# A graph attention and message kernel: VectorE adds a step's sums to its block one step later in its program

## The reference

```python
h = jnp.maximum(_layernorm(x), 0.0)
Q, K, V = (h @ Wq), (h @ Wk), (h @ Wv)            # each (6250, 8 heads, 32)
score = einsum('ehd,ehd->eh', Q[dst], K[src]) / sqrt(32) + relu(efeat @ W1 + b1) @ W2 + b2
m = segment_max(score, dst)
ex = exp(score - m[dst])
denom = segment_sum(ex, dst)
out = segment_sum((ex / denom[dst])[:, :, None] * V[src], dst)
x = x + out.reshape(n, 256) @ Wo + bo
```

## Time and profile before

| | |
|---|---|
| median of 3 runs | 5541.65 us (5539.95 to 5544.51) |
| span of the profiled execution | 6401.9 us |
| TensorE, VectorE, ScalarE, GpSimd busy | 73%, 54%, 52%, 53% of the span |
| fused stage in the profile | from about 280 to about 3280 us |

### The profile page before, as it was taken

The page is one execution under the profiler, slowest core; times in us unless marked ns, Lnnn a source line. Parts: engine busy times, 40 slices in busy tenths (PEclk is TensorE's granted clock), DMA queues, the critical chain, the costliest instruction groups (busy, mean ns, idle before and its releaser), DMA issues. The chain is left out here.

```text
span 6401.9 us, 106223 instructions
## 1 busy us (share of the span) xinstructions
PE 4687.5 (73%) x21476; PEld 2770.0 (43%) x21477; DVE 3466.9 (54%) x7990; ACT 3306.9 (52%) x8030; POOL 3423.4 (53%) x3416
## 2 busy tenths in 40 slices
PE   8788888888888888888789999545554445555555
PEld 5345445454444544445444444233333333333333
DVE  6487778888877887878853333222222222222224
ACT  3477777777777777777544444333333333333332
POOL 0366666666666666666610000466666666666665
PEclk9899999999999999999899999766666666666666
DMA  4466666766666666666644444333333333333334
GB/s 138 148 193 192 189 190 193 198 192 193 186 192 186 196 190 193 190 190 197 185 137 140 141 140 140 111 89 89 89 88 89 89 89 87 90 88 87 89 89 116
DMA packets 551965, 929.49 MB, mean 145 GB/s; under 512 B 112845, under 2 KB 361823, under 8 KB 551904
## 3 DMA queue, kind: packets, MB, share of 16 engines
q0 software_dynamic: 208384, 648.75, 36.3%
q1 hardware_dynamic: 343520, 280.03, 13.7%
HBM read 795.60 MB, written 132.88 MB: 145 GB/s over the span
## 5 line engine op out<-in xcount | busy, mean ns | idle before, releaser
L1006 POOL DMA_INDIRECT kv_rows<-kv_d,idx x1664 | 1751.9, 1053 | 1138.4 <-PE sums L1200 593.1
L1786 PE MATMUL m_sums<-m_rows,m_oh 128*128 x3328 | 1176.7, 512 | 1165.0 <-issue 908.6
L1723 POOL DMA_INDIRECT m_rows<-msg_d,m_idx x1568 | 1499.2, 956 | 854.8 <-issue 464.6
L1766 ACT ACTIVATE m_rows<-m_rows,m_norm 128x256 f32<-128x256 f32 x1568 | 710.8, 500 | 1628.9 <-DMA m_rows<-msg_d,m_idx 1528.2
L1786 PEld LDWEIGHTS m_sums<-m_rows,m_oh 128*128 128x128 f32 x3328 | 800.0, 256 | 1542.1 <-issue 1422.7
L1808 DVE TENSOR_TENSOR agg<-agg,m_sums 128x256 f32 x832 | 349.3, 420 | 1673.7 <-DMA kv_rows<-kv_d,idx 1005.8
L1200 PE MATMUL sums<-kv_rows,onehot 128*128 128x264 f32 x3328 | 984.3, 420 | 47.4 <-ACT onehot L1077 18.5
L1040 ACT ACTIVATE hid<-p_hid,b1s 128x512 f32<-128x512 f32 x784 | 495.6, 683 | 648.0 <-remote 226.9
L1200 PEld LDWEIGHTS sums<-kv_rows,onehot 128*128 128x128 f32 x3328 | 590.0, 197 | 461.8 <-issue 346.0
L1157 PE MATMUL p_q<-shelf,pickT 128*128 x4992 | 718.3, 281 | 56.8 <-ACT pickT L1063 28.2
L1656 PE MATMUL p_m<-wr,h1T 128*128 128x512 f32 x1568 | 710.1, 596 | 0.0
(11 more groups left out here) (194 smaller groups left out, 4459.9 us busy)
## 6 DMA issues: line engine op xcount, KB each, us to landing
msg_d<-msg SPq DMA_DIRECT2D x196, 512.0 KB, 2.9
dsts<-dstrow_d SPq DMA_DIRECT2D x208, 256.0 KB
ef_raw<-in_edge_attr_dram SPq DMA_DIRECT2D x195, 256.0 KB
kv_rows<-kv_d,idx POOLq DMA_INDIRECT x1664
m_rows<-msg_d,m_idx POOLq DMA_INDIRECT x1568
kv_d<-kvo SPq DMA_DIRECT2D x49, 260.0 KB, 2.1
pens<-pens_d SPq DMA_DIRECT2D x104, 96.2 KB
emlp<-mlp_d SPq DMA_DIRECT2D x104, 64.0 KB
```

What stands on the lines that cost most here:

```text
L1006: pool.indirect_dma_start(rows[:, u, k, :], None, kv_d[:, :], bass.IndirectOffsetOnAxis(idx[:, half, c:c + 1], 0)).then_inc(gathered[u], 16)
L1723: pool.indirect_dma_start(rows[:, u, k, :], None, msg_d[:, :], bass.IndirectOffsetOnAxis(idx[:, u // HALF, c:c + 1], 0)).then_inc(gathered ...
L1766: last = nc.scalar.activation(rows[:, u, k, :], rows[:, u, k, :], ACT.Copy, scale=norm[:, bass.ds(2 * g + k, 1)])
L1786: last = nc.tensor.matmul(sums[u % BANKS][:, 0:D], onehot[:, u % HOTS, k, :], rows[:, bass.ds(slot, 1), k, :].rearrange("p a d -> p (a d)" ...
```

## The change

In VectorE's program of the fused stage, the block that does `rescale` and `add` in step s now does them for step s - 13 (LATE + 2) and not for s - 12 (LATE + 1). The quads of block numbers are loaded where (u - 13) is a multiple of 4, and once more at the head of the body (u = 0), where the index into the quad is 3. Nothing else is changed: `weigh`, `dot`, the score chain and the programs of the other engines stay, with their waits.

```diff
-                    if is_step(s - LATE - 1):
-                        v = u - LATE - 1
-                        if v % LOADS == 0:
-                            behind = load_four(nc, dve, t["block"], s - LATE - 1, 0, BLOCKS - 1)
+                    if is_step(s - LATE - 2):
+                        v = u - LATE - 2
+                        if u == 0 or v % LOADS == 0:
+                            behind = load_four(nc, dve, t["block"], s - LATE - 2 - v % LOADS, 0, BLOCKS - 1)
                         if v % R == 0:
-                            rescale(s - LATE - 1, 2 * i + v // R, behind[0])
-                        add(s - LATE - 1, v % SLOTS, 2 * i + v // R, behind[v % LOADS])
+                            rescale(s - LATE - 2, 2 * i + v // R, behind[0])
+                        add(s - LATE - 2, v % SLOTS, 2 * i + v // R, behind[v % LOADS])
```

## The result

The changed kernel takes 5633.99 us in the median of 4 runs (5619.55 to 5637.19), the kernel before 5542.63 (5539.95 to 5544.51): a ratio of 1.0158, with a 95% interval of 1.0143 to 1.0172. That is 91 us more, where 67 less were forecast, and it is outside the forecast's range.

The account below looks back on a forecast made before the run. It took TensorE as fullest engine, with VectorE and TensorE waiting for each other in turns. Terms 0.32 + 0.20 + 0.10 + 0.12 - 0.10 = 0.64 us per chunk, x 104 = 67 us, gave 5475 us; range 5310 to 5560.

Parts of the forecast that it names:

- the sum of gains: Fused stage: expected cuts in TensorE's waits at `up`, `turn_drop`, `prod` and `score`, 0.74 us per chunk before the cost.
- What bounds the kernel: Fused stage: TensorE is fullest, and it and VectorE wait for each other in turns; a chunk takes 29.0 us.
- Term 1: TensorE's wait at `up`: 0.65 us per chunk goes, part comes back at `mlp_out` for `hid`; net gain 0.32.
- Term 2: TensorE's wait at `turn_drop`, 1.08 us per chunk: gain 0.20, as VectorE's own work leaves some wait.
- Term 3: TensorE's waits at `prod` (0.15 us per chunk) and `score` (0.24): gains of 0.10 and 0.12.
- Term 4: TensorE's `add_up` waits for an add that ends later: cost 0.10 us per chunk after `drop`, upper bound 1.7.
- rival E: TensorE waits 0.58 us for `added` in each of steps 2, 3 and 7: slower, 5645 us, chance 0.15.
- Term 5: VectorE's `load_four`, issued five times in 16 steps, not four: hidden in VectorE's idle time, cost 0.
- rival D: Collision of VectorE's two-input instructions with GpSimd's `weigh` turns costlier: 0.62 us more per chunk, 5539 us, chance 0.07.

Follow-up runs that it names:

- e4: The changed kernel with GpSimd's `weigh` two of its steps earlier: 5543.31 us, ratio to the kernel before 1.0001.
- e9: The kernel before with GpSimd's `weigh` two steps earlier: 5546.26 us, ratio 1.0006.
- e7: The kernel before with GpSimd's `weigh` between its step's two gathers and not behind them: 5592.58 us, ratio 1.0088.
- e2: The kernel before with TensorE's `add_up` of n waiting for the add of n-1, not of n-2: 5630.14 us, ratio 1.0158.
- e10: The changed kernel with GpSimd's `weigh` one of its steps later: 5683.69 us, ratio 1.0251.
- e8: The changed kernel with the moved add ahead of VectorE's `weigh`, and GpSimd's `weigh` two steps earlier: 5629.52 us, ratio 1.0150.
- e1: The kernel before, profiled again with no edit: one run of 5545.2 us, span 5543.3.
- e11: The kernel before with GpSimd's `weigh` two steps earlier and, in steps 1 and 2, `dot`'s head sums behind `chain` and `drop`: 5509.25 us, 0.9938.
- e6: The kernel before with TensorE's `add_up` waiting for the add of n-1 and GpSimd's `weigh` two steps earlier: 5559.73 us, ratio 1.0032.
- e5: The kernel before with four more block-number loads in 16 steps, each at a multiple of four: 5544.03 us, ratio 0.9997.
- e3: The kernel before with block-number loads moved to the changed kernel's steps, adds at their old place: 5616.08 us, ratio 1.0134.

## Why the prediction was wrong

The step that failed is the sum of gains, 0.74 us per chunk for waits of TensorE that the kernel before hardly has (e4 against e9 leaves 0.05%, inside the spread), together with the overlap of the second scan and GpSimd's `weigh`, which the sum put at nothing and which cost 91 us.

**The doses add up.** What VectorE's hit instructions take beyond their undisturbed time, times 104 chunks, against the time lost:

| run | excess per chunk | x 104 | lost |
|---|---|---|---|
| e4, changed kernel, weigh two steps earlier (scan alone) | 0 | 0 us | 0 us |
| e7, weigh between the gathers | 1.215 - 0.683 = 0.53 us | 55 us | 48 us |
| e2, tighter wait (15 us are its own) | 1.410 - 0.683 = 0.73 us | 76 us | 87 - 15 = 72 us |
| the changed kernel | 1.745 - 0.683 = 1.06 us | 110 us | 91 us |
| e10, weigh one step later | 0.72 + 0.70 = 1.43 us | 149 us | 141 us |

The estimates lie 6 to 21% above the losses, as they carry the window's mean over to all chunks: summed over all 104 scans of its trace, the excess in the changed kernel is 101 us and not 110. The table holds for instructions in the row from the score to `turn_drop`. `place`, in step 7, is outside it: its 0.16 us per chunk in e4 cost nothing that shows, and what its 0.51 in e8 cost is open.

**What bounds the kernel.** This step failed at its source. All the terms of the gain came from one trace that was 860 us longer than the runs. I noticed the difference and placed it in the last stage, by GpSimd's idle time there. Some 500 of it were in the fused stage: a chunk took 29.0 us there, against 2180 us for 90 scans, 24.2, in e1, and there are 104. The signals that came late for no visible reason are absent from e1.

**Term 1, `up`** (0.65 us, net 0.32): the kernel before has no such wait. Worth 0. **Term 2, `turn_drop`** (1.08, net 0.20): 0.35 is there, and the reasoning that VectorE's own row of work, not the add's wait, sets it was right: e4 leaves 33.0 us of it where e1 has 31.5. e11, which shortens that row, removes it. **Term 3**: 0.6 us in all for `prod`, and 0.14 per chunk at `score`. Worth 0 to 0.1.

**Term 4, the cost of the tighter wait** (0.10 per chunk, at most 1.7, and rival E): 15 us in e6, 0.15 per chunk. The size was right. Rival E had the sign and not the mechanism, so its 5645 us, near the 5634 measured, is luck: it named steps 2, 3 and 7 and a wait of `sums` for `shelf`, and that wait does not occur between 420 and 2600 us in the changed kernel; it stands only at the end of the stage, with 22.7 us (33 times) between 2600 and 2820.

**Term 5, the loads**: 0, and e5 bears that out.

**The collision, rival D.** The mechanism was there, with its line and its partner, at a chance of 0.07 and a price of 0.62 us per chunk; in the forecast's own sum it stood at nothing. Two numbers were wrong. The base was taken as 0.29 us per chunk from the disturbed trace, and is 0. The price of a hit was taken from one row as 0.91; in the changed kernel the mean over all chunks is 1.06. And D was set against a forecast gain of 0.64, which did not exist. With the right three numbers the same sum gives 0 + 1.06 x 104 = 110 us more; 91 were measured. I had also said that an earlier scan would hand the collision on to VectorE's `weigh`. It didn't: that instruction stayed at 0.70 us in the mean in the changed kernel. It isn't immune, though: in e9 six of its 728 took 2.17 us, each starting 0.50 to 0.51 us before GpSimd's `weigh`.

The Trainium skill, SBUF — State Buffer, section "SBUF: two separate sides", names the two parties rightly: in the lines shown VectorE and GpSimd hold each other up where a VectorE instruction with two SBUF inputs (or `first_node`) meets `weigh`, and the first scan, with one, is spared. By the page, whichever starts first has the port for its whole instruction and the other waits. The trace agrees with the whole instruction: a held scan ends 0.55 to 0.56 us after `weigh`, so nearly all of its 0.68 us is still to do, however early it had started; and in e1, where VectorE's `weigh` has the port, GpSimd's ends 0.94 us after it. On who started first the records mislead. Taken at their word e2 is against the page, since the scan starts 0.60 us before `weigh` and still waits; with a hold that reaches 0.7 us back, as e10 shows, it is not.

**What stays open.** Why the shift moves `weigh` by just that much. Before, `weigh` starts 2.26 us after the end of the score's last matmul (1514.54 to 1516.80); in the changed kernel's timeline 1.38 (1537.49 to 1538.87). The scans keep their distance from the score (0.57 and 0.48). GpSimd follows TensorE's `summed` and its own queue of gathers, and a longer chunk lets it catch up, so the collision may keep itself going once it is there. This was not tested by itself. That the changed kernel would be even without the collision is shown (e4, e9), but for the meetings with `place`; what pushed it over the 0.2 us of margin is not. Also open is why, in the kernel before, VectorE's `weigh`, which starts 0.27 us before GpSimd's (e1), isn't held: it follows the second scan, which starts 0.88 us before and so is ahead of the hold, without a gap.

## What to carry to other kernels

Compare the span of the profiled execution with the median before reading a single wait: if they differ by more than the runs do among themselves (0.4% here), have a second profile before pricing anything by the first. An engine's wait that disappears is worth nothing if another engine is at 97%; here 0.5 us per chunk of VectorE's idle time went and the time stayed at 0.0%, while e11, which took away the full engine's own wait of 31.5 us, gained 0.6%. And a shift in one engine's program moves what runs beside it on the others: list the pairs that hold each other up, measure the margin between their starts (0.88 us here, of which 0.66 were needed), look at the longest and shortest of an instruction and not at its mean alone, and move the one that nothing waits for (here GpSimd's weigh, two steps earlier) out of the way first.

## What the runs showed of the hardware

- A scan of 64 x 256 with both inputs in SBUF takes 0.68 us alone, and 1.7 to 2.3 us when it meets GpSimd's `weigh` (128 x 528, 1.08 us alone) in the changed kernel and e2; it then ends 0.55 to 0.56 us after `weigh`. VectorE's `weigh` did the same where it was held (2.17 us, 0.58 after, in e9). Where VectorE's has the port it stays at 0.68 us, and GpSimd's grows to 1.40 in the mean (e1).
- The hold begins before the profile's record of GpSimd's `weigh`: a scan is held if it starts up to 0.655 us before that record and spared from 0.663 on (all runs), a `first_node` of 0.27 us up to 0.698 and from 0.716 (e10). The record's start doesn't say who was first.
- The same held for instructions as small as 1 x 128 and 1 x 72: 0.27 and 0.29 us alone, 1.87 and 1.83 when held, 0.99 in the mean (e10). The first scan, whose second input comes from PSUM, stayed at 0.67 to 0.68 in every run, also in e7, where `weigh` started while it ran.
- Loading four numbers from SBUF into VectorE's registers took 0.34 us from a start at a multiple of four and 0.96 from one past it (medians, e5 and e3).
